# One layer of a language-model tower on one core: a bias added three heads later, an output-projection tile ahead of a score unit, key copies behind an exponential, and a new start of the token table

## The chip, the cores and the metric

The kernel runs on one core of a Trainium2 chip. Its metric is the device time in microseconds (us) of one execution. The core's engines run side by side, each in the order of its own queue: TensorE (PE) multiplies and transposes, VectorE (DVE), ScalarE (ACT) and GpSimd (POOL) work on tiles, SyncE (SP) issues DMAs. They wait for each other through semaphores.

## The reference, cut to what matters

```python
# x: (8, 512) token numbers under 2048; everything fp32
h = codebook[x]                                   # 256 wide
h = gelu(h @ W1 + b1) @ W2 + b2                   # 256 -> 1024 -> 256
n = layernorm(h)                                  # first 128 columns: token part, last 128: position part
q, k = n_pos @ Wq, n_pos @ Wk                     # 16 query heads and 4 key heads of 64, q rotated by an angle per head
v = n_tok @ Wv                                    # 4 value heads
att = q @ k.T / 8 + slope[head] * (i - j)         # causal
att = exp(att - max) / (1 + sum(exp(att - max)))
h = h + (att @ v) @ Wo
n = layernorm(h)
h = h + (gelu(n @ U1 @ V1 + c1) @ U2) @ V2 + c2   # rank 64, 1024 wide
```

## The kernel before

The first part, `token_table`, runs the token network once for each of the 2048 codebook rows, in 4 chunks of 512, and writes a table to DRAM: the row, the normalised position part, the values. Each fp32 operand is split into a high part (a copy on ACT) and a low part (a subtraction on DVE), and a product is three matmuls of such parts. A chunk has 8 steps. In a step PE makes the first product (lines 480 to 482, 6 matmuls), ACT does the gelu (line 305) and the high copy (line 310), DVE the low part (line 408), and two steps later PE makes the second product (lines 495 to 497, 12 matmuls). At the step with number 3 PE also transposes the next chunk's rows (line 467). `keep_rows` on DVE adds the second bias `b2_row`, for the first time at step 9. At step 6 ACT first copies a weight of the later layer (line 320), and it waits for eleven loads which POOL issues, the last of them `c2_row` (line 253).

The second part, `layer`, gathers the table's rows for 8 examples of 512 tokens and runs 16 heads for each example. The program is written in slots, one for each head: slot s holds head s mod 16 of example s / 16, and work of earlier heads and of the previous example is woven in. The order in each engine's queue is what sets the time of everything:

- PE: the three score units of the head (lines 1130 and 1131; units of 512, of 384 and 128, and of 256 keys), the products that `first(s)` names between the second and the third unit, in even slots the values of two earlier heads (line 1158), the third unit, the transposes of the weights of head s - 2 (line 1142, 10 matmuls) and the products that `second(s)` names.
- DVE: the reciprocals of the previous head (lines 917 and 919), then the biased scores with their minimum, a tile at a time (line 910, tiles of 512, 384, 128 and 256 keys), and before the last tile the low parts of what `first(s)` names. The row norm of the previous example's output has its front in slot 7 and its back in slot 9 (lines 888 to 899), behind the last tile.
- ACT: the move of transposed weights out of PSUM (line 787), the high copies of what `first(s)` names (queries line 797, keys line 802), then the four exponentials with their sums (line 780).
- POOL: the four scalings of the previous head's weights by the reciprocals (line 744), the gathers of the next example behind slot 1's scaling, and in slot 10 the addition of the second feed-forward bias `c2` to all rows of the previous example (line 770). It waits for the row norm, and the last sums of the feed-forward (slot 15) wait for it.

Keys of the next group come in slots 1, 5, 9 and 13, a pair of queries in even slots. The output projection of the previous example, `("w", b, t)`, has four tiles of 24 matmuls (line 1026), in slots 3 to 6, each at the end of its slot. The feed-forward runs as one burst in slot 12. The PSUM bank `a_bank` is shared by most single products, and `opened` makes a product wait until the use before it in `every` has been split:

```python
    home = {("x", 0, 0): c_bank, ("q", 0, 0): bank(4)}
    every = [("k", 0, 0)] + [use for s in range(SLOTS) for use in first(s) + second(s)]
```

The score units go through two banks in turn, and `ring_opened` makes a unit wait until DVE has read the one two before it.

## Time and profile before

| | before |
|---|---|
| time, median of 3 runs | 969.41 us (963.27 to 970.1) |
| the profiled execution | 972.13 us |
| its span, first to last instruction | 970.3 us |
| PE busy | 869.9 us, 90% of the span |
| ACT busy | 723.7 us, 75% |
| POOL busy | 630.2 us, 65% |
| DVE busy | 620.2 us, 64% |
| mean granted clock of PE | 0.970 |

The profiled execution's time is its span and 1.83 us around it. In the rows, a time in brackets is how long the engine stood idle just before, with what ended it. Matmuls are pipelined, so that one starts before the one ahead of it is over.

### The profile page before, as it was taken

The numbers are of one execution on the slowest core, as the hardware profiler recorded it, in microseconds if no ns is written. First come the engines' busy times: TensorE is split into PE (matmuls) and PEld (weight loads), VectorE is DVE, ScalarE is ACT, GpSimd is POOL, SyncE is SP. The second block draws the span as 40 slices with busy tenths as digits, with TensorE's granted clock in tenths as the row PEclk, the third lists the DMA queues.
The fourth block names the chain that finished last, engine by engine and source line by source line (L and its number), as shares of the span: only waits on it lengthen the run. The fifth ranks groups of instructions, "written<-read, shape, count | busy, mean of one in ns | idle before, by whom it ended". The sixth has DMA issues, their size and how long they took to land.

```text
span 970.3 us, 16896 instructions
## 1 busy us (share of the span) xinstructions
PE 869.9 (90%) x5552; PEld 676.4 (70%) x5552; DVE 620.2 (64%) x1898; ACT 723.7 (75%) x1611; POOL 630.2 (65%) x600
## 2 busy tenths in 40 slices
PE   6999658999989998999899998999899989998976
PEld 5888646777866686578657875787667766786663
DVE  4566636876685768575947584867566775668421
ACT  5754347998788867986889687968787788877813
POOL 6000068899685868587858876787759785768520
PEclk9999959999999999999999999999999999999997
DMA  9333350001000200020001000010001000000000
GB/s 258 67 109 109 115 189 2 1 2 55 2 1 2 76 1 1 1 78 1 1 1 57 22 1 1 23 56 1 1 23 55 2 1 23 1 2 1 1 22 22
DMA packets 23605, 33.55 MB, mean 35 GB/s; under 512 B 2608, under 2 KB 20176, under 8 KB 23520
## 3 DMA queue, kind: packets, MB, share of 16 engines
q1 hardware_dynamic: 19760, 19.01, 6.2%
q0 software_dynamic: 3760, 13.48, 4.9%
q8 instruction: 45, 0.74, 0.3%
q14 instruction: 40, 0.33, 0.1%
HBM read 17.80 MB, written 14.68 MB: 33 GB/s over the span
## 4 chain that ended last, share of the span: by engine, by line
PE 48%; DVE 15%; ACT 12%; issue 7%; POOL 5%; DMA 0%; DVEq 0%; POOLq 0%; ACTq 0%
PE ps L1026 14%; PE ps L1158 11%; PE ps L1142 6%; ACT probs L780 6%; DVE probs L910 5%; PE ps L1130 5%; PE ps L1110 4%; PE ps L1131 4%; POOL probs L744 3%; ACT turned_sb L787 3%; DVE sums L917 2%; DVE o_lo L962 2%; DVE xn L899 1%; PE ps L1104 1%; DVE q_both L927 1%
## 5 line engine op out<-in xcount | busy, mean ns | idle before, releaser
L744 POOL TENSOR_SCALAR probs<-probs,sums 128x512 f32<-128x512 f32 (+3 forms) x512 | 545.7, 1083 | 173.7 <-DVE sums L919 173.3
L910 DVE CUSTOM_DVE_ANT_0 probs<-ps,causal,slope 128x512 f32<-128x512 f32 (+3 forms) x512 | 260.0, 548 | 135.7 <-PE ps L1131 131.8
L780 ACT ACTIVATE probs<-probs,least 128x512 f32<-128x512 f32 (+3 forms) x512 | 282.1, 553 | 25.9 <-DVE least L910 19.0
L1130 PE MATMUL ps<-k_hi,q_both 128*128 128x512 f32 (+3 forms) x512 | 184.2, 360 | 28.1 <-DVE least L910 26.1
L787 ACT ACTIVATE turned_sb<-ps 128x1280 f32<-128x1280 f32 x128 | 157.2, 1228 | 69.6 <-PE ps L1142 69.5
L1158 PE MATMUL ps<-turned_sb,token_rows 128*64 128x512 f32 (+3 forms) x1024 | 152.0, 438 | 19.5 <-ACT turned_sb L787 19.4
L1142 PE MATMUL ps<-ident,probs 128*128 128x128 f32 x1280 | 163.0, 275 | 0.3
L1131 PE MATMUL ps<-k_lo,q_both 128*128 128x512 f32 (+3 forms) x512 | 153.5, 325 | 0.0
L1158 PEld LDWEIGHTS ps<-turned_sb,token_rows 128*64 128x64 f32 x1024 | 75.0, 136 | 104.6 <-issue 87.6
L1130 PEld LDWEIGHTS ps<-k_hi,q_both 128*128 128x128 f32 x512 | 97.8, 191 | 71.7 <-DVE least L910 45.7
L1142 PEld LDWEIGHTS ps<-ident,probs 128*128 128x128 f32 x1280 | 144.2, 141 | 1.5 <-POOL probs L744 1.3
L1131 PEld LDWEIGHTS ps<-k_lo,q_both 128*128 128x128 f32 x512 | 98.2, 192 | 5.0
L780 ACT ACTIVATION_READ_ACCUMULATOR probs<-probs,least 128x1 f32 x512 | 96.3, 188 | 0.0
L927 DVE TENSOR_TENSOR q_both<-ps,q_both 64x512 fp32r<-64x512 f32 x128 | 88.1, 688 | 9.7 <-ACT q_both L797 6.3
L797 ACT ACTIVATE q_both<-ps 64x512 fp32r<-64x512 f32 x128 | 75.4, 589 | 16.0 <-PE ps L1026 14.1
L259 POOL TENSOR_TENSOR row_guess<-row_var,row_power 128x4 f32<-128x4 f32 x4 | 4.1, 1026 | 94.6 <-DVE row_var L360 94.6
L1026 PE MATMUL ps<-wo_lo,o_hi 128*128 128x256 f32 x224 | 62.7, 280 | 0.0
L1026 PE MATMUL ps<-wo_hi,o_hi 128*128 128x256 f32 x224 | 62.7, 280 | 0.0
L1026 PE MATMUL ps<-wo_hi,o_lo 128*128 128x256 f32 x224 | 62.7, 280 | 0.0
L962 DVE TENSOR_TENSOR o_lo<-ps,o_hi 128x512 fp32r<-128x512 f32 x64 | 44.3, 691 | 21.1 <-ACT o_hi L829 20.3
L917 DVE TENSOR_SCALAR sums<-sums 128x4 f32<-128x4 f32 x128 | 41.9, 327 | 21.6 <-ACT probs L780 21.3
L408 DVE TENSOR_TENSOR hid_lo<-hid,hid_hi 128x512 fp32r<-128x512 f32 x32 | 22.1, 692 | 39.4 <-ACT hid_hi L310 28.1
(194 smaller groups left out, 1450.2 us busy)
## 6 DMA issues: line engine op xcount, KB each, us to landing
out_dram<-token_rows SPq DMA_DIRECT2D x7, 512.0 KB, 2.9
token_table<-made SPq DMA_DIRECT2D x4, 768.0 KB, 4.0
rows<-in_L_tok_codebook_dram SPq DMA_DIRECT2D x4, 512.0 KB, 9.3
w_f<-in_L_tok_W_dram SPq DMA_DIRECT2D x8, 256.0 KB, 5.0
early_rows<-made SPq DMA_DIRECT2D x4, 512.0 KB, 3.0
early_values<-xn SPq DMA_DIRECT2D x4, 512.0 KB, 3.0
token_table<-xn SPq DMA_DIRECT2D x4, 512.0 KB, 4.4
wo_f<-in_L_attn_Wo_dram POOLq DMA_DIRECT2D x1, 1024.0 KB, 11.1
```

The source lines that it names most:

```text
L744: ins = pool.tensor_scalar(at, at, recip[:, s % P_RING, q:q + 1], None, ALU.mult)
L780: act.activation(at, at, ACT.Exp, bias=least[:, s % P_RING, q:q + 1], scale=-1.0, accum_out=sums[:, s % P_RING, q:q + 1]).then_inc(exped, 1)
L787: act.activation(turned_sb[:, s % 2, :], turn_ps, ACT.Copy).then_inc(moved, 1)
L797: act.activation(q_both[at, s % 4, :], a_of("q", n, 0)[at, :], ACT.Copy).then_inc(q_high, 1)
L910: dve.tensor_tensor_reduce(out=probs[:, s % P_RING, at], in0=bank(unit % 2)[:, UNIT_AT[q]:UNIT_AT[q] + P * (q + 1)], in1=causal[:, at], sc ...
L927: dve.tensor_tensor(q_both[to, s % 4, :], a_of("q", n, 0)[at, :], q_both[at, s % 4, :].bitcast(F32), ALU.subtract).then_inc(q_low, 1)
L962: dve.tensor_tensor(o_lo[:, p % O_RING, :], o_bank, o_hi[:, p % O_RING, :].bitcast(F32), ALU.subtract)\
L1026: mm = pe.matmul(dst, w, x, start=n == 0, stop=n == len(parts) - 1)
L1130: pe.matmul(dst, w, k_hi[:, slot, 0:P * (q + 1)], start=True, stop=False)
L1131: mm = pe.matmul(dst, w, k_lo[:, slot, 0:P * (q + 1)], start=False, stop=True)
L1142: mm = pe.transpose(turn_ps[:, K_AT[k] + P * (q - k):K_AT[k] + P * (q - k + 1)], probs[:, s % P_RING, Q_AT[q] + P * k:Q_AT[q] + P * (k + 1 ...
L1158: mm = pe.matmul(o_bank[rows, P * k:T], v_rows[:, b % 3, k, n // REP * D:(n // REP + 1) * D], turned_sb[:, (s + e) % 2, K_AT[k]:K_AT[k] + ...
```

## The change

It has eight parts. The second feed-forward bias is added in slot 13 instead of slot 10. The first tile of the output projection moves from the end of slot 3 to between its second and third score units. The high copy of keys stands behind the head's first exponential instead of ahead of it. A product of queries or keys waits for the low part of its input only ahead of its last matmul. The second pair of queries gets a bank of its own. In the table's part the two biases have a semaphore each, ACT waiting for `b1` and DVE for `b2`. ACT's first instruction is a gelu on one column, which brings the gelu table in at the start. The tile of -0.5 is set once, and the semaphore `start` goes.

```diff
@@ token_table: SyncE, then ACT, then DVE
-                        .then_inc(b_in, 16)
+                        .then_inc(b1_in, 16)
...
-            sp.dma_start(b2_row[:, :], g["b2"].partition_broadcast(P)).then_inc(b_in, 16)
+            sp.dma_start(b2_row[:, :], g["b2"].partition_broadcast(P)).then_inc(b2_in, 16)
...
+            act.wait_ge(ident_done, 1)
+            act.activation(g["spare"][:, :], ident[:, 0:1], ACT.Gelu_apprx_tanh)
             ct_highs(0)
...
                 if n == 0:
-                    act.wait_ge(b_in, 32)
+                    act.wait_ge(b1_in, 16)
...
+                    if i == 0 and n == 0:
+                        dve.wait_ge(b2_in, 16)
@@ first(s) and second(s)
+    if 1 <= i < B and j == 1 + LAG:
+        out.append(("w", i - 1, 0))
     return out
...
-        if b < B - 1 and 1 + LAG <= j < 1 + LAG + NT:
+        if b < B - 1 and 1 + LAG < j < 1 + LAG + NT:
             out.append(("w", b, j - 1 - LAG))
@@ layer: banks
-    home = {("x", 0, 0): c_bank, ("q", 0, 0): bank(4)}
-    every = [("k", 0, 0)] + [use for s in range(SLOTS) for use in first(s) + second(s)]
+    home = {("x", 0, 0): c_bank, ("q", 0, 0): bank(4), ("q", 1, 0): c_bank}
+    every = [("k", 0, 0)] + [use for s in range(SLOTS) for use in first(s) + second(s) if use not in home]
@@ layer: POOL
-            pool.memset(minus_half[:, :], -0.5).then_inc(start, 1)
...
-            pool.wait_ge(start, 1)
...
-                if i >= 1 and j == 8 + LAG:
+                if i >= 1 and j == 11 + LAG:
                     b = i - 1
                     pool.wait_ge(xn_done, norm_no["y", b])
                     pool.tensor_tensor(h[:, b % 3, :, :], h[:, b % 3, :, :],
@@ layer: ACT
                 for use in first(s):
-                    high(*use)
-                for m in range(NT - 1):
+                    if use[0] != "k":
+                        high(*use)
+                if s < ALL:
+                    exps(s, 0)
+                for use in first(s):
+                    if use[0] == "k":
+                        high(*use)
+                for m in range(1, NT - 1):
@@ layer: DVE
-            dve.wait_ge(start, 1)
@@ layer: PE
-            def three(dst, pairs):
+            def three(dst, pairs, low_of_x=None):
+
                 parts = [x for (wh, wl), (xh, xl) in pairs for x in ((wh, xh), (wl, xh), (wh, xl))]
                 for n, (w, x) in enumerate(parts):
+                    if low_of_x and n == len(parts) - 1:
+                        pe.wait_ge(*low_of_x)
                     mm = pe.matmul(dst, w, x, start=n == 0, stop=n == len(parts) - 1)
...
-                    pe.wait_ge(x_low, b + 1)
+                    pe.wait_ge(x_high, b + 1)
```

ACT's queue at the start of the program, up to the first gelu and its copy, is this before (the high copies of the rows, then of the first weight by its four loads `w1_in`, then of the second weight):

```order
L268 ACT_TABLE_LOAD
L268 ACTIVATE ct_hi<-ps 128x512 [waits ct_full] x2
L289 ACTIVATE w_hi<-w_f 128x512 [waits w1_in0]
L289 ACTIVATE w_hi<-w_f 128x512 [waits w1_in1]
L289 ACTIVATE w_hi<-w_f 128x512 [waits w1_in2]
L289 ACTIVATE w_hi<-w_f 128x512 [waits w1_in3]
L299 ACTIVATE w_hi<-w_f 128x512 [waits w2_in0]
L305 ACT_TABLE_LOAD [waits hid_full]
L305 ACTIVATE hid<-ps,b_col 128x512 [waits b_in]
L310 ACTIVATE hid_hi<-hid 128x512 [waits hid_made]
```

and this now:

```order
L287 ACT_TABLE_LOAD
L287 ACTIVATE spare<-ident 128x1 [waits ident_done]
L268 ACTIVATE ct_hi<-ps 128x512 [waits ct_full] x2
L292 ACTIVATE w_hi<-w_f 128x512 [waits w1_in0]
L292 ACTIVATE w_hi<-w_f 128x512 [waits w1_in1]
L292 ACTIVATE w_hi<-w_f 128x512 [waits w1_in2]
L292 ACTIVATE w_hi<-w_f 128x512 [waits w1_in3]
L302 ACTIVATE w_hi<-w_f 128x512 [waits w2_in0]
L308 ACTIVATE hid<-ps,b_col 128x512 [waits hid_full,b1_in]
L313 ACTIVATE hid_hi<-hid 128x512 [waits hid_made]
```

The table load ahead of the first gelu is gone, the first of the program is now the gelu's, and the gelu waits for the first bias alone.

ACT's queue in slot 9 of the fourth example (the move, the copy of keys, the four exponentials, the next move) is this before:

```order
L787 ACTIVATE turned_sb<-ps 128x1280 [waits valued,turned]
L802 ACTIVATE k_hi<-ps 128x512 [waits scored,k_full]
L780 ACTIVATE probs,sums<-probs,least 128x512 [waits biased]
L780 ACTIVATE probs,sums<-probs,least 128x384 [waits biased]
L780 ACTIVATE probs,sums<-probs,least 128x128 [waits biased]
L780 ACTIVATE probs,sums<-probs,least 128x256 [waits biased]
```

and this now:

```order
L792 ACTIVATE turned_sb<-ps 128x1280 [waits valued,turned]
L785 ACTIVATE probs,sums<-probs,least 128x512 [waits biased]
L807 ACTIVATE k_hi<-ps 128x512 [waits scored,k_full]
L785 ACTIVATE probs,sums<-probs,least 128x384 [waits biased]
L785 ACTIVATE probs,sums<-probs,least 128x128 [waits biased]
L785 ACTIVATE probs,sums<-probs,least 128x256 [waits biased]
```

The key copy has gone behind the exponential of 512 keys; DVE's low part of the keys follows it.

POOL's queue around the bias, for the first example (four scalings are one head), is this before, in slots 10 and 11:

```order
L744 TENSOR_SCALAR probs<-probs,sums 128x128
L744 TENSOR_SCALAR probs<-probs,sums 128x256
L770 TENSOR_TENSOR token_rows<-token_rows,c_row 128x4x256 [waits xn_done]
L744 TENSOR_SCALAR probs<-probs,sums 128x512 [waits recip_done]
L744 TENSOR_SCALAR probs<-probs,sums 128x384
```

and this now, in slots 13 and 14:

```order
L751 TENSOR_SCALAR probs<-probs,sums 128x128
L751 TENSOR_SCALAR probs<-probs,sums 128x256
L775 TENSOR_TENSOR token_rows<-token_rows,c_row 128x4x256 [waits xn_done]
L751 TENSOR_SCALAR probs<-probs,sums 128x512 [waits recip_done]
L751 TENSOR_SCALAR probs<-probs,sums 128x384
```

The addition has gone behind twelve more scalings, those of heads 10, 11 and 12, and is otherwise the same.

## Rows read from the trace of the kernel before

**Rows 1.** The page, busy time of each engine (share of the span, instructions)
```profile
PE 869.9 (90%) x5552; PEld 676.4 (70%) x5552; DVE 620.2 (64%) x1898; ACT 723.7 (75%) x1611; POOL 630.2 (65%) x600
```

**Rows 2.** The timeline of heads 9 and 10 in the fourth example
```profile
471.57 0.75 DVE L910 CUSTOM_DVE_ANT_0 probs<-ps,causal,slope 128x512 f32<-128x512 f32 x1
472.52 0.60 ACT L802 ACTIVATE k_hi<-ps 128x512 fp32r<-128x512 f32 x1 [0.48 <-PE ps L1026]
473.01 0.72 ACT L780 ACTIVATE probs<-probs,least 128x512 f32<-128x512 f32 x1
473.15 0.69 DVE L931 TENSOR_TENSOR k_lo<-ps,k_hi 128x512 fp32r<-128x512 f32 x1
476.82 0.63 PE L1034 MATMUL ps<-ident,xn 128*128 128x128 f32 x4 [0.99 <-DVE xn L899]
```

**Rows 3.** The timeline of head 11 in the third example
```profile
379.57 2.37 POOL L770 TENSOR_TENSOR token_rows<-token_rows,c_row 128x1024 f32<-128x1024 f32 x1
380.22 1.75 DVE L917 TENSOR_SCALAR sums<-sums 128x4 f32<-128x4 f32 x1
382.12 0.75 DVE L910 CUSTOM_DVE_ANT_0 probs<-ps,causal,slope 128x512 f32<-128x512 f32 x1
382.94 0.39 PE L1130 MATMUL ps<-k_hi,q_both 128*128 128x256 f32 x1 [1.95 <-DVE least L910]
```

**Rows 4.** By stretch: busy (count) of PE, PEld, DVE, ACT, POOL; PEclk, DMA, GB/s
```profile
15.40:18.80 3.40, 3.15 (x8) 2.58 (x9) 2.05 (x4) 3.25 (x7) 3.40 (x4) 0.50 1.08 291
379.70:387.70 8.00, 6.05 (x29) 5.21 (x28) 4.96 (x13) 4.29 (x12) 6.50 (x5) 0.79 0.00 0
481.40:489.40 8.00, 6.06 (x36) 5.00 (x34) 5.85 (x15) 5.98 (x14) 6.53 (x5) 1.00 0.00 0
```

**Rows 5.** Line 917 from 270 us on: count, ns min/median/max
```profile
L917 DVE TENSOR_SCALAR sums<-sums x103: 154/170/1746, 274.0 to 920.7; 128x4 f32<-128x4 f32 x103
```

**Rows 6.** The timeline of GpSimd, head 13 of the fourth example
```profile
508.13 4.26 POOL L744 TENSOR_SCALAR probs<-probs,sums 128x512 f32<-128x512 f32 x4 [9.55 <-DVE sums L919]
```

**Rows 7.** The timeline of PE, head 10 in the third example
```profile
375.10 0.63 PE L1034 MATMUL ps<-ident,xn 128*128 128x128 f32 x4 [1.52 <-DVE xn L899]
```

**Rows 8.** The timeline of head 3 in the fourth example
```profile
433.94 0.39 PE L1130 MATMUL ps<-k_hi,q_both 128*128 128x256 f32 x1 [0.81 <-DVE least L910]
432.95 7.62 POOL L744 TENSOR_SCALAR probs<-probs,sums 128x512 f32<-128x512 f32 x7
437.29 1.31 PE L1142 MATMUL ps<-ident,probs 128*128 128x128 f32 x10
```

**Rows 9.** The timeline of the opening: start, us, engine, line, what, idle before
```profile
11.80 1.28 ACT L305 ACT_TABLE_LOAD   x1 [0.98 <-PE ps L482]
14.91 0.69 ACT L305 ACTIVATE hid<-ps,b_col 128x512 f32<-128x512 f32 x1 [1.83 <-DMA b_row<-in_L_tok_b_dram]
15.65 0.80 PE L480 MATMUL ps<-ct_hi,w_hi 128*128 128x512 f32 x1 [2.36 <-ACT hid L305]
16.89 0.63 POOL L253 DMA_DIRECT2D c_row<-in_L_ffn_b_dram  x1
20.00 0.39 PE L480 MATMUL ps<-ct_hi,w_hi 128*128 128x512 f32 x1
21.39 1.04 PE L467 MATMUL ps<-ident,rows 128*128 128x128 f32 x8
33.78 0.40 ACT L320 ACTIVATE y_hi<-wv_f 128x256 fp32r<-128x256 f32 x1
```

**Rows 10.** DMA issues: the feed-forward's second bias, KB, us to landing
```profile
c_row<-in_L_ffn_b_dram POOLq DMA_DIRECT2D x1, 128.0 KB, 13.5
```

**Rows 11.** The timeline where the layer begins
```profile
132.61 0.69 DVE L935 TENSOR_TENSOR pos_lo<-ps,pos_hi 128x512 fp32r<-128x512 f32 x1 [7.19 <-ACT pos_hi L805]
133.36 0.80 PE L1026 MATMUL ps<-pos_hi,wk_hi 128*128 128x512 f32 x1 [1.41 <-DVE pos_lo L935]
145.52 0.80 PE L1026 MATMUL ps<-pos_hi,wk_hi 128*128 128x512 f32 x1 [1.75 <-DVE q_both L927]
```

More of the change, by code:

```diff
@@ L78, in lm_tower @@
         vals = xn
+        minus_half = sb("minus_half", [P, NT])
         spare = sb("spare", [P, 1])
@@ L130, in token_table @@
     row_stats, row_mv = sb("row_stats", [P, NT, 6]), sb("row_mv", [P, NT, 2])
-    var, guess, tmp, power = (sb("row_var", [P, NT]), sb("row_guess", [P, NT]), sb("row_tmp", [P, NT]),
-                              sb("row_power", [P, NT]))
+    var, guess, tmp, power = sb("row_var", [P, NT]), sb("row_guess", [P, NT]), sb("row_tmp", [P, NT]), g["minus_half"]
     tok_hi, tok_lo, wv_hi, wv_lo, tokens, vals = (g["tok_hi"], g["tok_lo"], g["wv_hi"], g["wv_lo"], g["tokens"],
@@ L136, in token_table @@
     w1_in, w2_in = [sem(f"w1_in{k}") for k in range(2 * KD)], [sem(f"w2_in{k}") for k in range(4)]
-    rows_in, b_in = [sem(f"rows_in{n}") for n in range(2)], sem("b_in")
+    rows_in, b1_in, b2_in = [sem(f"rows_in{n}") for n in range(2)], sem("b1_in"), sem("b2_in")
     ang_in, wq_in, rest_in, idx_in, early_in = sem("ang_in"), sem("wq_in"), sem("rest_in"), sem("idx_in"), sem("early_in")
@@ L626, in layer @@
     var, guess, tmp = sb("var", [P, NT]), sb("guess", [P, NT]), sb("tmp", [P, NT])
-    minus_half = sb("minus_half", [P, NT])
+    minus_half = g["minus_half"]
     pos_hi, pos_lo = sb("pos_hi", [P, 2, T], F32R), sb("pos_lo", [P, 2, T], F32R)
@@ L643, in layer @@
     y_bank = (c_bank, a_bank)
-    start, rows_in, stored = sem("start"), sem("rows_in"), sem("stored")
+    rows_in, stored = sem("rows_in"), sem("stored")
     first_rows_in, first_values_in = sem("first_rows_in"), sem("first_values_in")
@@ L1068, in product @@
                     b = n // PAIRS
-                    pe.wait_ge(x_low, b + 1)
-                    three(a_of("q", n, 0), [((g["wq_hi"][:, cols], g["wq_lo"][:, cols]), (pos_hi[:, b % 2, :], pos_lo[:, b % 2, :]))])\
+                    pe.wait_ge(x_high, b + 1)
+                    three(a_of("q", n, 0), [((g["wq_hi"][:, cols], g["wq_lo"][:, cols]), (pos_hi[:, b % 2, :], pos_lo[:, b % 2, :]))],
+                          (x_low, b + 1))\
                         .then_inc(q_full, 1)
@@ L1073, in product @@
                     b, c = divmod(n, KVH)
-                    pe.wait_ge(x_low, b + 1)
-                    three(a_bank, [((both(g["wk_hi"], c), both(g["wk_lo"], c)), (pos_hi[:, b % 2, :], pos_lo[:, b % 2, :]))])\
+                    pe.wait_ge(x_high, b + 1)
+                    three(a_bank, [((both(g["wk_hi"], c), both(g["wk_lo"], c)), (pos_hi[:, b % 2, :], pos_lo[:, b % 2, :]))],
+                          (x_low, b + 1))\
                         .then_inc(k_full, 1)
```

## Prediction

> **What bounds the kernel.** I read the page's busy times first: PE works for 869.9 of 970.3 us, the others for 620 to 724 [rows 1]. So PE's queue sets the time, and an edit is worth what it takes from, or adds to, the idle time ahead of PE's instructions. PE's idle time is about 100 us. I then read the timeline slot by slot and asked at each PE gap what ended it. In examples 2 to 8 a slot has no gap at all where output-projection tiles give PE plenty to do (slots 4 to 7). The gaps are in slots 2, 3 and 8 (under 1 us), in slot 10, where PE waits 0.99 us for the row norm [rows 2], and in slot 11, where it waits 1.95 us for DVE [rows 3]. That one is the largest that returns. The view of stretches shows one thing more: PE's granted clock is 0.79 over 8 us around slot 11 in the third example and 1.00 in the fourth [rows 4]. So I looked at all seven: four are at 0.79 (examples 3, 5, 6 and 8), three at 1.00.
>
> **The bias, slot 10 to slot 13.** What holds PE in slot 11 is DVE: the unit may not start before the tile of line 910 at 382.12 is done, and that one stood behind line 917. Line 917 works on 4 columns. Its median is 0.17 us, and here it takes 1.75, from 380.22 to 381.97; the bias addition on POOL runs from 379.57 to 381.94 [rows 3, 5]. The small operation ends when the large one does, in all seven examples (six of 1.73 to 1.75, one of 1.40). That isn't a semaphore wait, since the operation is already running. So the addition costs DVE 1.75 - 0.17 = 1.58 us, and DVE is what PE waits for. Is all of it PE's? Without it the tile at 382.12 would start at about 380.5, and PE would be free at 381.0 and wait until 381.4, a gap of 0.4 in place of 1.95. ACT waits for the same tile and moves with it. So the whole 1.58 counts, 6 x 1.58 + 1.23 = 10.7 us. In its new place the addition stands behind head 12's scaling. POOL is then idle for 9.55 us, until 508.13 [rows 6], because PE is in the feed-forward burst, and DVE is idle for nearly as long: 2.37 us fit in without touching either. The sums that need it come two slots later. If that cover were missing it would cost the same 1.58 there as here.
>
> **The clock.** After the 1.95 us gap PE's clock fell in four of seven examples; it is at one half for (1.00 - 0.79) x 8 / 0.5 = 3.4 us each time [rows 4]. Work in that stretch takes twice as long, so at most 1.7 us are lost; PE waits for some of it, and I take 1.4, in all 5.6 us. The next longest gap of these examples, 1.52 us in slot 10 of the third [rows 7], was not followed by a fall. With a gap of 0.4 I expect no falls here. The range of this term is 0 to 6.8. The spread of the timed runs, 963.27 to 970.1, is of this size: it may be falls that came or didn't. The Trainium skill (TensorE: Matmul & The Clock Gate, What's actually happening) says that the gate's window is free-running and doesn't start with the kernel. By that rule which gaps are caught is chance, as three of seven here show, and falls may land at other gaps after the change: then this term is nothing, and the time is that of rival 1.
>
> **Key copies behind the first exponential.** In slots 1, 5, 9 and 13. ACT gains the wait for PE ahead of the copy (0.48 in slot 9), but DVE's low part of the keys comes later. In slot 9 the copy started at 472.52. Now the exponential starts when the tile of line 910 ends, 472.32, and takes 0.72 with 0.60 of the copy behind it, so the copy ends at 473.66 and the low part starts at 473.70 instead of 473.15: 0.55 later [rows 2]. Behind it on DVE stand the head's last tile and then, in slot 9 alone, the back of the row norm, whose result PE waits for at 476.82 with a gap of 0.99. So PE loses 0.55 there in seven examples: 3.9 us. Bounds: 0.2 if the norm's operations then meet fewer of POOL's scalings, and 1.2 if they meet more: in the third example the same gap is 1.52 without any change of order [rows 7], so such a meeting costs some 0.6. In slots 1, 5 and 13 nothing waits for the low part but the last tile and with it the fourth exponential and the next move; gain and loss there are within 0.15 of each other, and in slot 1 POOL hides them (next part). I take 0 for these.
>
> **The projection tile ahead of the third unit.** PE waits 0.81 us in slot 3 for DVE before that unit; the 24 matmuls, ready by then, would fill this. But behind them stand the transposes of head 1, which need POOL. POOL scaled that head from 432.95 for 4.26 us, until 437.21, held up by the four gathers ahead of it, and the transposes start at 437.29 [rows 8]. They were bound by POOL already. So the gap moves from ahead of the unit to ahead of the transposes and the gain is 0 in examples 2 to 7, up to 0.3 in one of them. The last example has no gathers, and gains about 0.4. What comes later is the fourth exponential of head 3, some 2 us; its scaling isn't due until POOL has done two heads more. It is also cover: a loss of 0.15 in slot 2 vanishes in the wait.
>
> **The opening.** The first gelu waited until 14.91 for the load of the second bias. The table load at 11.80 was hidden under that wait, and PE stood idle 2.36 us before 15.65 [rows 9]. Now the gelu can start at 11.80, provided the table is in: hence the early gelu, which alone would give nothing, while without it 1.28 would stay. PE then goes on without a gap. Also, after that idle time its clock was 0.50 until 18.80 [rows 4]. From 15.65 to 21.39 are two first products and one second: at the speed of 20.00 to 21.39, 1.39 for a first product, and as much for a second (twelve of half the width), that is 4.2 and not 5.7. Together 2.36 + 1.5, and 4.0 with what was overlapped at the edges. What is late next: the rows for the transposes at 21.39 are ordered behind the second bias, which landed before 14.91; they have to be there by 17.4. And line 320, at 33.78, would now be reached at 29.8, while `c2_row`, issued at 16.89, lands 13.5 later, at 30.4 [rows 9, 10]; ACT waits 0.6 there, and has about that much slack at each of the next steps. If neither cover holds, 2.8 remain. I take 4.0.
>
> **The layer's start.** Keys may start when the high part is there: the low part takes 0.69, and PE's start at 133.36 waited for it; 0.7 gained, as only the third matmul needs it. The second keys waited 1.75 at 145.52 for the split of the second queries in the same bank [rows 11]; that wait goes, but DVE's reciprocals and the next head's tile are only about 0.7 ahead of where they were, so 0.7 and not 1.75. The memset and `start` give 0.1. Together 1.5 (1 to 2.5).
>
> **The sum**, against the profiled 972.13: bias 10.7, clock 5.6, opening 4.0, layer's start 1.5, last example 0.4, together 22.2 gained; 3.9 lost in slot 10. 972.13 - 18.3 = 953.8 us. The median of the runs shown is 2.7 below the profiled execution; if it had fewer falls of the clock, part of the clock's term isn't to be had against it, but the time after is the same.
>
> **Rivals.**
> 1. The falls stay. Some other gap, the one of 1.5 in slot 10 above all, is followed by the fall that slot 11's was. 953.8 + 5.6 = 959.4. For it: gap and fall are only together in four of seven, and slot 10's gap grows. Against: the gap of 1.52 was followed by none. 0.15.
> 2. The row norm runs into POOL. It stands on DVE 0.55 later, while POOL scales heads 7 and 8; if each example loses 1.2 in place of 0.55 and the clock falls in slot 10 besides (gap over 2), that is 7 x (0.65 + 1.4) = 14 more: 968. With the collision alone, 958.4, which the range has. The whole of it: 0.05.
> 3. Line 917's 1.75 us aren't the bias's doing, and it stays long; then bias and clock give nothing: 953.8 + 16.3 = 970.1, no change. Against it speak seven equal endings and a median of 0.17. 0.04.
> 4. Slower. The projection tile's 24 matmuls put the third unit, the last tile, the fourth exponential and the reciprocals of head 3 about 2.8 us later. If DVE's queue behind the reciprocals is then late for head 4, PE waits 2.8 in each of seven examples. Together with rival 3 that is 970.1 + 19.6 = 990. It turns slower than before once the loss in slots 3 and 4 is over 18.3 / 7 = 2.6 us an example, all else as forecast: 973.4 at the full 2.8. Against it: DVE waited for this very tile's sum anyway before the reciprocals of head 3, so they come no later than now. 0.03.
> 5. More than forecast: the norm loses nothing in slot 10 (950) and the layer's start gives its upper end: 949. 0.08.
>
> The forecast, 951 to 958, has 0.65.
>
> **Range.** 948 to 962: rival 5, the forecast and rival 1 with its bounds; left out are rivals 2 to 4 and the edges. About 1% is what a measurement of this kernel can tell from no change, 959.7 to 979.1. The forecast, rival 5 and most of rival 1 lie under it: faster by over 1% 0.89, within 1% (rivals 2 and 3) 0.09, slower 0.02, since rival 4 has to come with rival 3 for that.
>
> **What would show it.** Line 917 in slot 11 at about 0.2 us and PE's gap there at 0.4 to 0.7; the bias on POOL in front of its long idle time; clock 1.00 around slot 11. In slot 10 PE's gap for the row norm at about 1.55. In slot 3 no gap ahead of the third unit, and one of 0.7 ahead of the transposes. The first gelu at 11.8, the transposes of the second chunk at about 17.4. The prediction is wrong if line 917 is long without the bias beside it, if the bias now holds someone in slot 13, or if new falls of the clock appear.

## The result, and the profile after

| | before | after |
|---|---|---|
| time, median | 968.94 us (4 runs, 963.27 to 970.1) | 953.51 us (4 runs, 952.84 to 954.45) |
| ratio, 95% interval | | 0.9836 [0.9811, 0.9861] |
| the profiled execution, its span | 972.13, 970.3 us | 954.45, 952.6 us |
| mean granted clock of PE | 0.970 | 0.977 |

The kernel is 1.6% faster, and the interval of the ratio lies wholly below 1; forecast were 953.8 us. The page's busy times of the kernel after:

```profile
PE 865.0 (91%) x5552; PEld 670.9 (70%) x5552; DVE 607.5 (64%) x1898; ACT 728.7 (76%) x1611; POOL 629.7 (66%) x599
```

PE does the same 5552 matmuls in 4.9 us less [rows 1]; that fewer of them run at half clock fits this, with the mean granted clock up from 0.970 to 0.977. DVE's 12.7 us less are the wait inside line 917 (now line 928) that has gone: its 128 instructions took 41.9 us before and 29.0 after. Line numbers are up by at most 15: scores 1145, transposes of the weights 1157, tiles with minimum 921, sums 928, low keys 942.

The timeline of head 11 in the third example, after:

```profile
375.11 0.16 DVE L928 TENSOR_SCALAR sums<-sums 128x4 f32<-128x4 f32 x1
375.50 0.75 DVE L921 CUSTOM_DVE_ANT_0 probs<-ps,causal,slope 128x512 f32<-128x512 f32 x1
376.31 0.39 PE L1145 MATMUL ps<-k_hi,q_both 128*128 128x256 f32 x1 [0.43 <-DVE least L921]
```

The small operation takes 0.16 us in place of 1.75 and PE waits 0.43 in place of 1.95 [rows 3]. Measured from score unit to score unit, slot 11 has gone from 6.16, 7.48, 6.17, 7.64, 7.60, 6.14 and 7.40 us to 4.63 to 4.65 (4.92 once), 15.8 us less in seven examples. The three that were 6.1 to 6.2 have lost 1.5 (1.25 where it is 4.92), the four at half clock 2.8 to 3.0.

GpSimd's timeline at the bias's new place, fourth example, then the stretch that answers to [rows 4]:

```profile
489.98 2.38 POOL L775 TENSOR_TENSOR token_rows<-token_rows,c_row 128x1024 f32<-128x1024 f32 x1
499.47 1.56 POOL L751 TENSOR_SCALAR probs<-probs,sums 128x512 f32<-128x512 f32 x1 [7.11 <-DVE sums L930]
```

```profile
373.70:381.70 8.00, 7.40 (x46) 6.11 (x46) 5.80 (x19) 6.84 (x15) 5.43 (x6) 1.00 0.00 0
```

The addition uses up 2.4 of GpSimd's 9.5 idle microseconds [rows 6], and the clock's column reads 1.00 where it read 0.79.

Slot 10 has become longer. Head 9 and 10 of the fourth example, after:

```profile
465.13 0.58 ACT L807 ACTIVATE k_hi<-ps 128x512 fp32r<-128x512 f32 x1
465.75 0.69 DVE L942 TENSOR_TENSOR k_lo<-ps,k_hi 128x512 fp32r<-128x512 f32 x1 [0.56 <-ACT k_hi L807]
466.89 0.44 PE L1145 MATMUL ps<-k_hi,q_both 128*128 128x384 f32 x1 [0.40 <-DVE least L921]
467.94 1.38 DVE L910 TENSOR_SCALAR xn<-token_rows,mv,guess 128x256 f32<-128x256 f32 x4
469.46 0.63 PE L1047 MATMUL ps<-ident,xn 128*128 128x128 f32 x4 [1.03 <-DVE xn L910]
```

DVE stands idle 0.56 us for the high part of the keys. The gap ahead of the norm's transposes is 1.03, where it was 0.99 [rows 2], but there is a new one of 0.40 a little earlier: the head's second score unit waits for DVE to read the bank, because the last tile of head 9 stands behind the low keys. Measured from the head's first unit to its second, that is 1.11 us in place of 0.56. Slot 10 is 0.60 longer in five examples, 0.07 and 0.39 in the other two, 3.5 in all.

The opening and the layer's start, after:

```profile
11.81 0.69 ACT L308 ACTIVATE hid<-ps,b_col 128x512 f32<-128x512 f32 x1 [0.30 <-PE ps L487]
13.64 0.63 PE L487 MATMUL ps<-ct_lo,w_hi 128*128 128x512 f32 x1
14.80 0.39 PE L487 MATMUL ps<-ct_lo,w_hi 128*128 128x512 f32 x1
18.53 0.71 PE L472 MATMUL ps<-ident,rows 128*128 128x128 f32 x5
...
129.77 0.79 PE L1039 MATMUL ps<-pos_hi,wk_hi 128*128 128x512 f32 x1 [0.69 <-ACT pos_hi L810]
145.86 0.80 PE L1039 MATMUL ps<-pos_hi,wq_hi 128*128 128x512 f32 x1 [2.41 <-DVE k_lo L942]
```

The first gelu starts at 11.8 and PE has no gap behind it, both as forecast [rows 9]. But its matmuls still take 0.63 us up to the one that starts at 14.06, and 0.39 only from 14.80 on, and the second chunk's transposes start at 18.53, 2.86 earlier than before and not 4.0. PE's first product of keys starts 0.7 earlier behind its input [rows 11]. Its wait of 1.75 for the split of the second queries has gone. In the next slot it waits 2.41 for the low part of the keys, where before it waited 1.59:

```profile
150.42 0.50 PE L1026 MATMUL ps<-pos_hi,wq_hi 128*128 128x512 f32 x1 [1.59 <-DVE k_lo L931]
```

### The profile page after: what moved, and what is told of

It reads as the page before. It is cut to its first block, busy times and chain, and to the rows that moved or that the text cites. A ratio compares the mean times of both kernels' runs of the same rounds, so it can differ in the third digit from the quotient of the medians.

```text
span 952.6 us, 16893 instructions
## 1 busy us (share of the span) xinstructions
PE 865.0 (91%) x5552; PEld 670.9 (70%) x5552; DVE 607.5 (64%) x1898; ACT 728.7 (76%) x1611; POOL 629.7 (66%) x599
## 4 chain that ended last, share of the span: by engine, by line
PE 41%; DVE 13%; POOL 13%; ACT 10%; issue 10%; DMA 0%; DVEq 0%; POOLq 0%; ACTq 0%
PE ps L1039 11%; POOL probs L751 10%; PE ps L1173 9%; PE ps L1157 5%; DVE probs L921 5%; PE ps L1145 4%; PE ps L1125 4%; ACT probs L785 4%; PE ps L1146 3%; ACT turned_sb L792 3%; POOL token_rows L739 3%; DVE o_lo L973 2%; PE ps L1119 1%; ACT q_both L802 1%; DVE xn L910 1%
## 5 line engine op out<-in xcount | busy, mean ns | idle before, releaser
L1145 PE MATMUL ps<-k_hi,q_both 128*128 128x512 f32 (+3 forms) x512 | 183.1, 358 | 20.5 <-DVE least L921 18.3
L1173 PE MATMUL ps<-turned_sb,token_rows 128*64 128x512 f32 (+3 forms) x1024 | 152.0, 438 | 13.4 <-ACT turned_sb L792 13.4
L259 POOL TENSOR_TENSOR row_guess<-row_var,minus_half 128x4 f32<-128x4 f32 x4 | 4.1, 1026 | 91.1 <-DVE row_var L365 91.1
L824 ACT ACTIVATE ff<-ps,c_col 128x512 f32<-128x512 f32 x64 | 40.1, 692 | 7.8 <-PE ps L1120 7.6
```

Of the source, the lines that this page charges most:

```text
L1145: pe.matmul(dst, w, k_hi[:, slot, 0:P * (q + 1)], start=True, stop=False)
L1173: mm = pe.matmul(o_bank[rows, P * k:T], v_rows[:, b % 3, k, n // REP * D:(n // REP + 1) * D], turned_sb[:, (s + e) % 2, K_AT[k]:K_AT[k] + ...
```

## The experiments

Twelve kernels ran, in four groups. Kernels of one group share their runs of the kernel before, whose medians were 969.62, 969.3, 970.15 and 969.2 us.

### The bias alone

```diff
@@ kernel before, layer: POOL
-                if i >= 1 and j == 8 + LAG:
+                if i >= 1 and j == 11 + LAG:
```

> The kernel before with one edit: the second feed-forward bias is added on GpSimd in slot 13, not in slot 10. My theory: the addition alone held up the 4-column operation of VectorE at the start of slot 11 (1.75 us in place of 0.17), TensorE waited for it 1.95 us, and that gap let TensorE's clock fall in four of seven examples. Then this one edit gives 10.7 for the wait and 5.6 for the clock, 16.3 in all: 972.1 - 16.3 = 955.8 profiled, some 953 in the median, the small operation at 0.2 us in all seven slots 11, a TensorE gap of 0.4 there, and no stretch at half clock behind it. Rival A, the small operation is late for another reason (the scalings or slot 11 itself): no change, 968 to 970. Rival B, the wait goes but the clock's falls have another cause: 958 to 959, with stretches at half clock elsewhere in slots 10 to 13.

Measured: 952.23 us (950.02 to 954.39, 5 runs), ratio 0.9818 [0.9799, 0.9838]. The sums' line and PE's wait in slot 11 of the third example:

```profile
L917 DVE TENSOR_SCALAR sums<-sums x128: 154/169/658, 138.6 to 900.3; 128x4 f32<-128x4 f32 x128
375.01 0.38 PE L1130 MATMUL ps<-k_hi,q_both 128*128 128x256 f32 x1 [0.44 <-DVE least L910]
```

No operation of 1.75 us is left, and slot 11 is 4.63 to 4.66 us in six examples (4.93 once). Rivals A and B fall. This one line gives 17.4 us; the whole change gives 15.4, and the two intervals overlap. So what the other seven parts give and take cancels, within what these runs can tell.

### The same place, another form of the small operation

```diff
@@ kernel before, layer: a 1 beside each sum, then DVE
+            step(dve.memset(sums[:, :, :, 1], 1.0))
...
-                step(dve.tensor_scalar(recip[:, s % P_RING, :], sums[:, s % P_RING, :], 1.0, None, ALU.add))
+                step(dve.tensor_reduce(recip[:, s % P_RING, :], sums[:, s % P_RING, :, :], mybir.AxisListType.X, ALU.add))
```

> The kernel before, with the bias still in slot 10 as one operation, and one edit on VectorE: the 4-column sum + 1 at the head of each slot is no longer a tensor_scalar from SBUF to SBUF. Each sum has a constant 1 beside it, and a tensor_reduce over the pair adds them, 4 x 2 elements in, 4 out. Theory A: the small operation is held by its form. A tensor_scalar whose input and output both lie in SBUF has to have what the running GpSimd operation holds, a reduction does not. Then it takes about 0.2 us in slot 11 beside the bias, TensorE's gap there is 0.4 to 0.5, no stretch at half clock follows, and the time is that of the kernel with the bias in slot 13, 952 (950 to 954). By the Trainium skill (SBUF - State Buffer, Who interferes with whom) tensor_reduce never contends on this chip; this is the rule that theory A takes up. Theory B: whatever VectorE starts from SBUF while a GpSimd operation with two operands runs is held up: the reduction takes 1.75 us as well, and the time stays at 968 to 970.

Measured: 952.86 us (950.54 to 953.96, 6 runs), ratio 0.9828 [0.9796, 0.9861], the same as with the bias moved. Slot 11 of the third example, with the bias still there:

```profile
375.19 2.39 POOL L770 TENSOR_TENSOR token_rows<-token_rows,c_row 128x1024 f32<-128x1024 f32 x1
375.86 0.15 DVE L917 TENSOR_REDUCE recip<-sums 128x4 f32<-128x8 f32 x1
376.05 0.18 DVE L919 RECIPROCAL recip<-recip 128x4 f32<-128x4 f32 x1
377.05 0.39 PE L1132 MATMUL ps<-k_hi,q_both 128*128 128x256 f32 x1 [0.43 <-DVE least L910]
```

The reduction runs through in 0.15 us while GpSimd's addition is on. Over all 128 heads it takes 0.147 to 0.165, never more, where the tensor_scalar took 0.154 to 1.746. Theory B falls. The edit changes a second thing, for the old operation worked in place and the reduction writes another tile. That isn't the cause: the reciprocal, which works in place on four elements, runs through in 0.18 us at 376.05, with the addition still on until 377.58. What collided was neither the engines as such nor the place but the form of the instruction: a tensor_scalar from SBUF to SBUF. By the Trainium skill (SBUF — State Buffer, Who interferes with whom) VectorE and GpSimd share a pair of SBUF ports as an exclusive lock held for the whole instruction; a tensor_scalar in its two-port mode needs it and a reduction on this chip doesn't. The rows agree with both, 1.75 us and 0.15; that this tensor_scalar runs in the two-port mode no trace here shows.

### The bias in quarters

```diff
@@ kernel before, layer: POOL, slot 10
+                    for t in range(NT):
+                        ins = pool.tensor_tensor(h[:, b % 3, t, :], h[:, b % 3, t, :], g["c2_row"][:, :], ALU.add)
```

> The kernel before with one edit: the bias stays in slot 10, but is added in four operations on 128 x 256 elements (one for each row of tokens in a partition) in place of one on 128 x 4 x 256. It tells what the small VectorE operation waits for. Theory A: it starts its work only when the GpSimd operation that is running has ended. Then it lasts at most one quarter, about 0.6 us, in place of 1.75; TensorE's gap in slot 11 falls from 1.95 to some 0.8, the falls of the clock go, and the time is 972.1 - 7 x 1.1 - 5.6 = 959, 955 to 961. Theory B: additions of two full operands on GpSimd slow VectorE for as long as they last, one or four: the small operation stays at 1.7, and the time at 968 to 970.

Measured: 956.54 us (955.45 to 959.85, 5 runs), ratio 0.9858 [0.9836, 0.988]. Slot 11 of the third example:

```profile
375.58 2.80 POOL L771 TENSOR_TENSOR token_rows<-token_rows,c_row 128x256 f32<-128x256 f32 x4
376.23 0.81 DVE L917 TENSOR_SCALAR sums<-sums 128x4 f32<-128x4 f32 x1
378.01 0.39 PE L1130 MATMUL ps<-k_hi,q_both 128*128 128x256 f32 x1 [1.01 <-DVE least L910]
```

A quarter takes 2.80 / 4 = 0.70 us, so quarters end at about 376.28, 376.98 and so on; the small operation, which started at 376.23, ends at 377.04, just behind the second. It is so in five of the seven examples. In the fourth it starts in the middle of the second quarter and ends behind it, after 0.45 us. In the second example it isn't held at all:

```profile
277.24 0.16 DVE L917 TENSOR_SCALAR sums<-sums 128x4 f32<-128x4 f32 x1
278.44 0.38 PE L1130 MATMUL ps<-k_hi,q_both 128*128 128x256 f32 x1 [0.43 <-DVE least L910]
```

There it starts 0.055 us ahead of the second quarter; in the five it starts 0.04 to 0.05 ahead. Theory A holds: it waits for the end of one GpSimd instruction, not for the end of the work. PE's gap is 1.01 to 1.03 in six examples, and no half-clock stretch follows in any.

### One slot later

```diff
@@ kernel after, layer: POOL
-                if i >= 1 and j == 11 + LAG:
+                if i >= 1 and j == 12 + LAG:
```

> The kernel after with the bias one slot later, in slot 14. It tests the cover of its place, the only thing that slot 13 has and others lack. In the trace with the bias in slot 13 the scalings of head 13 end at 502.1 and the small VectorE operation of the next head starts at 502.7, so the bias would run from 502.1 to 504.4 and hold it for about 1.7 us; TensorE's gap of 0.4 before the next unit would be about 2.1. My theory: 7 x 1.6 = 11 us slower than after, and if gaps of this length let the clock fall, up to another 1.4 in half of them: 964.7 to 970. Rival: the small operation was late in slot 11 because of heads' work there and not of the bias; then the time is that of after within 1 us.

Measured: 972.12 us (968.9 to 974.43, 10 runs), ratio 1.0035 [1.0012, 1.0059]. Fourth example, then the eight microseconds that follow in the third and in this one:

```profile
506.62 2.37 POOL L775 TENSOR_TENSOR token_rows<-token_rows,c_row 128x1024 f32<-128x1024 f32 x1
507.27 1.75 DVE L928 TENSOR_SCALAR sums<-sums 128x4 f32<-128x4 f32 x1
509.99 0.38 PE L1145 MATMUL ps<-k_hi,q_both 128*128 128x256 f32 x1 [1.94 <-DVE least L921]
```

```profile
408.00:416.00 8.00, 8.00 (x46) 6.21 (x45) 4.98 (x14) 5.06 (x12) 7.04 (x8) 0.79 0.21 69
509.00:517.00 8.00, 7.01 (x37) 6.13 (x39) 5.50 (x20) 4.12 (x11) 7.34 (x7) 0.79 0.20 68
```

The rows of slot 11 [rows 3, 4] have come back in slot 15: slot 15 goes from 4.44 us to 5.94 in the first of six examples and to 7.23 to 7.55 in the other five, where the clock falls; 16.7 in all. The seventh, in the last example, has no slot behind it: its gap is 1.94, no fall follows, and that example's end is 2.5 us longer. My theory named the mechanism and underpriced it at 11 to 16. The cover that the prediction named for slot 13 is worth 18.6 us.

```diff
@@ the bias in slot 14, and the reduction in place of the tensor_scalar, as above
```

> The kernel with the bias in slot 14 (972.1), where the small tensor_scalar of slot 15 took 1.75 us beside it, with the tensor_reduce over pairs in place of the tensor_scalar. If the form of the small operation is what is held up, in whatever slot, the time is that of after, 953.5 (951 to 955), with the reduction at about 0.2 us beside the bias, TensorE's gap in slot 15 at 0.4 and no stretch at half clock behind it. If anything else in slot 15 suffers from the bias, part of the 18.6 us stays: over 958.

Measured: 955.05 us (952.69 to 956.27, 4 runs), ratio 0.9847 [0.9819, 0.9874]. Fourth example:

```profile
503.29 2.39 POOL L775 TENSOR_TENSOR token_rows<-token_rows,c_row 128x1024 f32<-128x1024 f32 x1
503.95 0.16 DVE L928 TENSOR_REDUCE recip<-sums 128x4 f32<-128x8 f32 x1
505.16 0.38 PE L1147 MATMUL ps<-k_hi,q_both 128*128 128x256 f32 x1 [0.43 <-DVE least L921]
```

All six slots 15 are 4.44 or 4.45 us. 17 of the 18.6 us are back with the form of one operation changed. In this execution slot 10 of the third example takes 10.10 us in place of 8.4, at half clock behind a gap of 1.21:

```profile
366.00:370.00 4.00, 2.79 (x13) 1.50 (x13) 3.86 (x15) 3.12 (x7) 2.51 (x3) 0.83 0.01 4
370.00:374.00 4.00, 4.00 (x26) 2.26 (x23) 1.86 (x7) 2.17 (x7) 2.87 (x4) 0.75 0.00 0
```

### Keys first

```diff
@@ kernel after, layer: ACT
                 for use in first(s):
-                    if use[0] != "k":
-                        high(*use)
-                if s < ALL:
-                    exps(s, 0)
-                for use in first(s):
-                    if use[0] == "k":
-                        high(*use)
-                for m in range(1, NT - 1):
+                    high(*use)
+                for m in range(NT - 1):
```

> The kernel after with one edit undone: the high copy of the keys stands ahead of the head's first exponential again. My theory: behind the exponential it costs about 0.5 us in slot 10 of seven examples, since VectorE's row norm comes later, and gives nothing in slots 1, 5 and 13; so this kernel is 3.5 (2.8 to 4.2) faster than the one after, 950.0, with TensorE's gap ahead of the transposes in slot 10 at 0.99 again in place of 1.44. Rival: the loss in slot 10 is real but the other three slots gain as much, so that undoing it changes nothing (953 to 954), and slots 1, 5 and 13 are then 0.1 to 0.2 longer each.

Measured: 948.7 us (947.88 to 951.63, 5 runs), ratio 0.978 [0.976, 0.98]; nothing measured was faster. That is 4.8 below the median of the kernel after, where 3.5 (2.8 to 4.2) was expected. Slot by slot against the kernel after, slot 10 is 0.60 to 0.62 shorter in six examples and 0.07 in the last, slot 2 0.12 shorter in six, slot 3 0.10 longer in five, slot 14 0.08 longer in six; the profiled spans are 3.5 us apart. The expectation put the whole of it in the gap ahead of the norm's transposes; 0.55 of each 0.60 is in the earlier start of head 10's second unit (0.55 behind the first in place of 1.11; the gap of 0.40 isn't there now). The rival falls: slots 1, 5 and 13 and their neighbours give and take about 0.1 each.

> The kernel after with the key copies ahead of the first exponential again, and with the same tensor_reduce in place of the small tensor_scalar. In the kernel before this operation took 0.34 us in the mean of 103, against a median of 0.17, of which 0.10 is slot 11's; the rest is held up by the scalings of slots 2, 8 and 10. If these delays lie on the path, the kernel gains on the 948.7 us of the same kernel with tensor_scalar: I expect 1 to 3 us less, 947. Rival: VectorE has slack there and the time is the same within 1 us.

Measured: 949.59 us (948.21 to 951.14, 6 runs), ratio 0.9803 [0.9771, 0.9835]: the same as keys first alone. DVE has slack wherever a scaling held up the small operation, save beside the bias; slot 9 is 0.18 shorter and slot 10 0.19 longer. The rival was right.

### The opening

```diff
@@ kernel before, token_table: b_in split into b1_in (ACT) and b2_in (DVE), and
+            act.wait_ge(ident_done, 1)
+            act.activation(g["spare"][:, :], ident[:, 0:1], ACT.Gelu_apprx_tanh)
```

> The kernel before with the opening's part of the change alone: a semaphore for each of the two biases, and the early gelu on one column that brings the table in at the start. From the trace after, the rows' transposes of the second chunk come 2.86 us earlier than before, and the products of the fourth chunk also 2.86, so I expect 2.9 (2.5 to 3.2) less than before: 966. Rival, the prediction's own term of 4.0: 965. Rival, the gain is eaten at the start of the layer by what is loaded there (the gathers of the first example wait for the table's last rows): under 1.

Measured: 970.03 us (967.19 to 973.23, 12 runs), ratio 1.0008 [0.9993, 1.0024]. Then the same on the kernel with the bias in slot 13:

> The kernel before with the bias in slot 13 (952.2) and the opening's part of the change besides. On the kernel before the opening's part showed no gain, 970.0 beside 969.6, but the falls of the clock in slot 11 blur a difference of 1 us there; here they are gone. In the four profiled executions with the old opening the second chunk's transposes start 16.6, 13.5, 13.8 and 13.6 us after TensorE's first instruction, and in eight with the new one at 12.6 to 13.8, in the mean 13.1. My theory: the profile of before was an exception, where the second bias landed 1.6 us later than in the other three, and the opening's part is worth 0.5 to 1: 951.2 to 951.7, TensorE's first matmuls at half clock until 12 to 14.5 whatever the order. Rival: the prediction's term of 4.0, or the 2.9 of the two profiles, is what a usual execution gains: 948.2 to 949.3.

Measured: 952.66 us (951.39 to 954.15, 6 runs), ratio 0.9836 [0.981, 0.9862], beside 952.23 without it. No gain in either place. The reason is in the opening of the kernel with the bias alone, whose opening is that of before:

```profile
11.94 1.28 ACT L305 ACT_TABLE_LOAD   x1 [0.42 <-PE ps L482]
13.32 0.69 ACT L305 ACTIVATE hid<-ps,b_col 128x512 f32<-128x512 f32 x1
18.39 0.82 PE L467 MATMUL ps<-ident,rows 128*128 128x128 f32 x6
```

The gelu follows the table load at once: the second bias had landed, at 13.30. In the other two kernels with the old opening, the quarters and the reduction, the gelu waited 0.21 and 0.27 for it, until 13.56 and 13.69. Only in the execution of [rows 9] did it come at 14.91, some 1.2 to 1.6 us later. Counted from PE's first instruction, the second chunk's transposes start at 16.6 in that one and at 13.5, 13.8 and 13.6 in the others; with the new opening at 12.5 to 13.8 in nine. What spreads these is the clock: the last of PE's first matmuls that takes 0.63 us starts at 11.2 in one execution (tile back, below) and at 14.1 in another (the kernel after), and whoever starts earlier runs more of them slowly. Where that last slow matmul starts 8.45 us behind PE's first instruction with the old opening (bias alone) and 8.47 with the new one (this kernel), the transposes start 13.5 and 13.4 behind it: no difference.

> The kernel after without the gelu on one column that brings the table in. My theory: the table is then loaded when the first gelu is reached, 1.28 us, with nothing in front of it to hide it, so the first gelu starts 1.28 later after the end of its product than in the kernel after, and the second chunk's transposes come 1.3 later after the first instruction of TensorE (13.9 where clean runs of the early gelu show 12.6). Rival: ScalarE reaches the first gelu before its product is done and the load is hidden, as the first bias's wait hid it before: no difference.

Measured: 953.19 us in one run. The gelu is 1.28 later, the transposes start 13.4 behind PE's first instruction, inside the range of the others. What the early gelu gives is under what one run can show.

### The layer's start, and the projection tile

```diff
@@ keys first, with these undone
-    home = {("x", 0, 0): c_bank, ("q", 0, 0): bank(4), ("q", 1, 0): c_bank}
+    home = {("x", 0, 0): c_bank, ("q", 0, 0): bank(4)}
...
-                    pe.wait_ge(x_high, b + 1)
+                    pe.wait_ge(x_low, b + 1)
```

> The kernel after with the keys copied first (948.7) and with the layer's start as before: a product of keys or queries waits for the low part of its input ahead of its first matmul again, and the second pair of queries shares the bank. Against the kernel before it then has the bias in slot 13, the opening's part and the projection tile. My theory: the earlier first product gives 0.7 and the bank of its own little, because TensorE then waits 2.4 to 2.6 us for the low part of the keys in slot 2 instead; so this is 0.7 to 1.3 slower than 948.7: 949.4 to 950. The opening and the tile are then what separates it from the kernel with the bias alone (952.2): some 2.5. Rival: both waits counted, 2.0 or more slower, 951 to 952, and the opening gives nothing, as the opening's part alone on the kernel before showed none (970.0 beside 969.6).

Measured: 949.84 us (948.83 to 951.93, 5 runs), ratio 0.9794 [0.9773, 0.9816]; 1.1 slower than 948.7 in the medians, and the two kernels' ranges overlap, so neither my 0.7 to 1.3 nor the rival's 2.0 is settled by the times. The traces tell more. From the second chunk's transposes to the first score unit this kernel takes 116.30 us and the one with keys first 115.57; in all seven traces with the old start of the layer it is 115.8 to 116.3, in the seven with the new one 115.0 to 115.7. So the start gives about 0.7. Example 1 is 0.8 longer here, with one stretch of 10.2 us at half clock in place of one of 3.4, and the end of the program is 1.4 shorter, with 10.2 us at half clock in place of 13.7. That end, from the last head's first unit on, takes 52.2 to 55.0 us in kernels that don't differ there, so one or two microseconds between two medians say little. For this reason it stays open, too, why this kernel is 2.8 faster than the one with the opening and the bias (952.66), from which the projection tile and the tile of -0.5 set it apart: slot by slot, the projection tile's 0.65 is all that can be put down to them.

```diff
@@ kernel after, first(s) and second(s): the tile ("w", i - 1, 0) back at the end of slot 3
```

> The kernel after with the first projection tile at the end of slot 3 again. By the trace after, slot 3 became 0.10 shorter in six examples and 0.65 in the last, slot 2 0.12 longer in six. If the tile is the cause of slot 3's gain alone, undoing it gives slots 3 their lengths of before (0.10 and 0.65 longer) and leaves slot 2; the loss in slot 2 then belongs to the key copies in slot 1. Rival: slot 2's 0.12 belongs to the tile's new place in the order of the banks and goes with it.

Measured: 951.23 us in one run. Slots 2 and 3 keep their lengths within 0.02 in examples 2 to 7, and slot 3 of the last is 0.65 longer. So the tile gives 0.65 once and nothing else; the 0.10 of slot 3 and the 0.12 of slot 2 in the other examples come from the keys' order, as the kernel with keys first shows from the other side. Of my expectation, the 0.65 and slot 2 held and the 0.10 of slot 3 didn't; the rival falls.

## Why the prediction came out

**What bounds the kernel** was read rightly: the two largest changes that recur are in the slots named, 11 and 10, and slots 4 to 7 of examples 2 to 8 moved by at most 0.03.

**The bias and the clock**, 10.7 + 5.6 = 16.3 forecast, 15.8 in the traces of before and after and 17.4 in the medians of the bias alone. The small operation's 1.58 us, the gap of 0.4, the place on GpSimd and the clock at 1.00 came as written. The mechanism was taken from seven equal endings; the reduction and the quarters show it. Rival 3 is excluded: with the bias in slot 13 no small operation is over 0.66 us, and with the bias left in place, another form of the small operation gives the same time.

**The clock's falls** came behind 13 of 21 gaps of 1.92 to 1.97 us (4 of 7 before, 4 of 7 with the opening alone, 5 of 7 with the bias in slot 14) and behind none of the gaps of 0.4 to 1.0 that stand in slot 11 otherwise. Slot 10, with gaps of 1.0 to 1.5, had one fall in 98. That the gap brings the fall is shown by the reduction, which leaves the bias where it was, takes away the gap, and has none. So rival 1 is real and rare, and its 5.6 us didn't come. Why one gap of 1.95 is caught and the next isn't stays open.

**Key copies**, 3.9 forecast in slot 10, 3.5 there and 3.5 between the profiled spans (4.8 between the medians). The size held and the place didn't: the step "Behind it on DVE stand the head's last tile and then, in slot 9 alone, the back of the row norm, whose result PE waits for" skipped that PE waits for the last tile too. Head 10's second unit is 0.55 later, just the delay forecast for the low part, and what PE does ahead of the norm's transposes is 0.55 later with it. So the gap there stayed at 1.03. From the last tile's start to these transposes it is 3.06 us before and 3.10 after: the norm's four large operations took 1.38 in place of 1.67, and the small ones ahead of them about as much more.

**The opening** is the step that failed: 4.0 forecast, 2.9 in the profiled pair, nothing in the medians. Its wait was read off one execution in which a DMA landed late: 7.4 us from issue to landing, and 5.5 to 6.8 in the other thirteen traces. The part of 1.5 for the clock assumed that PE would be at full clock once it didn't wait. In that execution the last slow matmul ahead of the wait starts at 11.5, in the one after at 14.1. The profiled time of before stood 2.7 above the median, which the prediction put down to falls of the clock. The late bias is as large: the second chunk's transposes are 2.8 to 3.1 later than in the other three with the old opening. That it makes up the 2.7 isn't shown, since the other runs of before have no trace.

**The layer's start**, 1.5 forecast: 1.2 in the traces of before and after, 0.7 of it ahead of the first score unit and 0.5 in example 1, and 1.1 between two kernels' medians. The first product's 0.7 holds in all traces. The wait for the shared bank did go, and DVE was next: PE waits 0.8 longer for the low keys in slot 2. The half-clock stretch in slot 2, 6.8 us in the profiled execution after, isn't a new fall, for before has one of 3.4 in the same place. Each of the 14 traces has one that begins between 140.8 and 147.4 us; they last 3.4 to 10.2 us with the old start of the layer and 3.4 to 6.8 with the new one. So example 1 can't be read to better than a microsecond or two.

**The projection tile**: 0.65 in the last example (0.4 forecast), nothing in the others. In slot 3 the gap moved as written, from ahead of the third unit to 0.95 ahead of the transposes, for which GpSimd is needed [rows 8]. Rival 4 didn't come. Fourth example, after:

```profile
429.28 1.31 PE L1157 MATMUL ps<-ident,probs 128*128 128x128 f32 x10 [0.95 <-POOL probs L751]
```

That the total came within 0.3 us is luck; that it came near is not. The bias and the clock, 16.3 of the 22.2 forecast as gained, were right in size and cause. The rest cancelled: measured against medians, the opening gave 4.0 less than forecast, and the base was 2.7 lower than the profiled execution from which 18.3 was taken.

## What to carry to other kernels

Where a tiny operation on VectorE lasts many times its median, look at which GpSimd instruction ends when it does: move the GpSimd instruction into a stretch in which VectorE has nothing of that form, cut it up, or give the tiny operation a form that doesn't collide (here a reduction over pairs in place of a tensor_scalar). An edit that moves a long GpSimd instruction needs its new neighbours checked, as one slot more cost 18.6 us. A stall at the start of a program, seen in one execution and ended by a DMA, should be priced from several.

## What the runs showed of the hardware that was not expected

A reduction of 8 into 4 elements took 0.14 to 0.17 us in 384 heads of three kernels, whatever GpSimd did, and a tensor_scalar on 4 elements from 0.15 to 1.76. The order of the two engines' work matters to a few hundredths of a microsecond: in quarters, the one small operation that started 0.055 ahead of the next quarter ran through, and those that started 0.04 to 0.05 ahead waited out a further 0.70. In different executions of much the same opening PE's first matmuls take 0.63 us up to one that starts at 11.2 or as late as 14.1, and 0.39 from then on; the column of the granted clock reads 1.00 over 9.0 to 12.4 us in all of them, and only the matmuls' own durations show it.
